# Five tiles of the choice of experts in the first stage instead of six, and five one-hot blocks weighted by VectorE instead of ten

## The reference, cut to what matters

```
x = x + attention(layernorm(x), ctx, ctx)                  # 16 heads, 512 x 512 scores
h = layernorm(x); xn = rmsnorm(h) * norm_w
q = (xn @ wq) as [token, 8 heads, 2, 128]
sim = q . keys                                             # [2, token, head, 64 keys]
s1, i1 = top_k(sim[0], 16);  s2, i2 = top_k(sim[1], 16)
all_scores = s1[:, None] + s2[None, :]                     # 256 per head
final_scores, pk = top_k(all_scores, 16);  final_idx = (i1 * 64 + i2)[pk]
hidden = gelu(xn . expert_down[final_idx]) * relu(final_scores)
x = x + sum over heads and k of hidden * expert_up[final_idx]
```

## Time and profile before

| | |
|---|---|
| median of 3 runs | 1234.25 us (1229.91 to 1236.24) |
| the profiled execution, its span | 1233.31 us, 1231.5 us |
| PE busy | 1062.0 us, 86% |
| PEld busy | 731.2 us, 59% |
| DVE busy | 948.9 us, 77% |
| ACT busy | 393.8 us, 32% |
| POOL busy | 615.3 us, 50% |
| mean granted clock of PE | 0.922 |

### The profile page before, as it was taken

The page is one execution under the profiler, slowest core; times in us unless marked ns, Lnnn a source line. Parts: engine busy times, 40 slices in busy tenths (PEclk is TensorE's granted clock), DMA queues, the critical chain, the costliest instruction groups (busy, mean ns, idle before and its releaser), DMA issues.

```text
span 1231.5 us, 28859 instructions
## 1 busy us (share of the span) xinstructions
PE 1062.0 (86%) x10152; PEld 731.2 (59%) x10152; DVE 948.9 (77%) x4836; ACT 393.8 (32%) x717; POOL 615.3 (50%) x772
## 2 busy tenths in 40 slices
PE   4899987878878777057998999999999999999998
PEld 2444443323212323036787887888878888888887
DVE  4757554968998999669899999998989989953310
ACT  2257544433444353013222222222222222222211
POOL 6320410332210313225777787877877696877511
PEclk9799998888787798556999999999999999999999
DMA  5344313221221110180010000000100010000000
GB/s 166 116 149 143 106 44 121 66 72 49 83 73 47 34 43 6 47 318 3 1 30 16 16 26 17 20 25 11 39 12 25 2 34 16 26 15 24 2 18 9
DMA packets 59924, 63.76 MB, mean 52 GB/s; under 512 B 6882, under 2 KB 56164, under 8 KB 59268
## 3 DMA queue, kind: packets, MB, share of 16 engines
q1 hardware_dynamic: 59780, 61.90, 15.7%
HBM read 42.21 MB, written 19.66 MB: 50 GB/s over the span
## 4 chain that ended last, share of the span: by engine, by line
PE 53%; DVE 27%; POOL 7%; issue 6%; DMA 3%; SPq 2%; ACT 2%; DVEq 0%; POOLq 0%; ACTq 0%
PE bank L1282 50%; DVE mem L1201 4%; PE bank L1285 3%; POOL mem L792 2%; DVE mem L1137 2%; DVE mem L1238 2%; DVE mem L1084 2%; DVE mem L1083 2%; SPq L492 2%; DVE mem L1088 1%; DVE mem L1133 1%; DVE mem L1140 1%; DVE mem L1080 1%; DVE mem L1092 1%; DVE mem L1120 1%
## 5 line engine op out<-in xcount | busy, mean ns | idle before, releaser
L1282 PE MATMUL bank<-mem 128*128 128x32 bf16 (+5 forms) x9672 | 1012.4, 276 | 100.2 <-DVE mem L1201 35.7
L1282 PEld LDWEIGHTS bank<-mem 128*128 128x128 bf16 (+3 forms) x9672 | 679.0, 123 | 382.9 <-issue 175.8
L792 POOL TENSOR_TENSOR mem<-mem 128x1536 bf16<-128x1536 bf16 x118 | 325.7, 2761 | 156.2 <-DVE mem L1235 151.9
L1201 DVE TENSOR_REDUCE mem<-bank 128x1 f32<-128x512 f32 x256 | 167.9, 682 | 87.1 <-PE bank L1282 86.8
L908 ACT ACTIVATE mem<-bank 128x512 f32<-128x512 f32 x256 | 149.0, 601 | 207.9 <-PE bank L1282 207.0
L1238 DVE TENSOR_TENSOR mem<-mem,bank 128x2048 bf16<-128x2048 bf16 x128 | 155.4, 1214 | 0.0
L1285 PE MATMUL bank<-mem 128*128 128x128 f32 (+3 forms) x480 | 75.9, 290 | 66.0 <-POOL mem L704 25.0
L1285 PEld LDWEIGHTS bank<-mem 128*128 128x128 f32 (+3 forms) x480 | 54.9, 142 | 113.8 <-issue 71.0
L799 POOL TENSOR_TENSOR mem<-mem 128x512 f32<-128x512 f32 x64 | 83.5, 1305 | 50.5 <-ACT mem L947 50.5
L958 ACT COPY mem<-bank 128x512 f32<-128x512 f32 x128 | 74.9, 585 | 104.8 <-PE bank L1282 104.8
L673 POOL TENSOR_TENSOR mem<-mem 128x32 f32<-128x32 f32 (+5 forms) x224 | 45.7, 242 | 117.7 <-DVE mem L1092 117.7
(11 more groups left out here) (103 smaller groups left out, 764.1 us busy)
## 6 DMA issues: line engine op xcount, KB each, us to landing
mem<-parts_d SPq DMA_DIRECT2D x192, 64.0 KB, 2.3
parts_d<-mem SPq DMA_DIRECT2D x16, 384.0 KB, 2.6
mem<-in_L_ffn_expert_down SPq DMA_DIRECT2D x16, 256.0 KB, 3.0
downT_d<-mem SPq DMA_DIRECT2D x16, 256.0 KB, 3.2
mem<-downT_d SPq DMA_DIRECT2D x4, 1024.0 KB, 8.5
mem<-in_L_ffn_expert_up SPq DMA_DIRECT2D x4, 1024.0 KB, 16.7
tok_d<-mem SPq DMA_DIRECT2D x16, 160.0 KB, 1.8
mem<-tok_d SPq DMA_DIRECT2D x16, 160.0 KB, 2.4
```

The lines of the kernel that those rows point to most:

```text
L792: nc.gpsimd.tensor_tensor(ow[q % 2], i0, i1, ALU.mult).then_inc(ow_rdy, 1)
L1201: nc.vector.tensor_reduce(nmx[g % 2][:, i % TB, i // TB:i // TB + 1], psum[n % 3][:, :], AX.X, ALU.max, negate=True).then_inc(s_max, 1)
L1282: return nc.tensor.matmul(o, l, r, start=first, stop=last)
```

## The change

NA goes from 6 to 5: tile 5's tasks, similarities, transposition and store leave the first stage, and every wait that counts tiles from NA moves along. The first run of the second stage has five tiles (5 to 9) where it had four (6 to 9); the loop starts at the same tile, 10. OWN keeps the blocks 2, 5, 8, 11 and 14, where it had 1, 2, 4, 5, 7, 8, 10, 11, 13 and 14; POOL weights eleven blocks of the first chunk, where it weighted six.

```diff
         SLOTS = NG + 5
-        NA = 6
+        NA = 5
...
-        OWN = [q for q in range(16) if q % 3 != 0]
+        OWN = [q for q in range(16) if q % 3 == 2]
...
         def runs(eng, run):
-            run(-1, 3, NA, 4, -1)
+            run(-1, 3, NA, 5, -1)
             with eng.Fori(0, 2) as i:
-                run(i * 2 + 2, 2, i * 3 + (NA + 4), 3, None)
+                run(i * 2 + 2, 2, i * 3 + (NA + 5), 3, None)
```

## The result

The changed kernel takes 1254.47 us (median of 4 runs, 1249.45 to 1256.92), the kernel before 1233.89 in the same comparison: 1.0159 times as long, 95% interval 1.0111 to 1.0208. A second comparison, with 6 and 23 runs, gave 1249.1 against 1234.54: 1.0107 (1.0078 to 1.0135). The change makes the kernel slower by 13 to 21 us; forecast were 23 (1257 against 1234), in a range of 1246 to 1267. Both medians lie in the range. The two profiled executions, spans of 1231.5 and 1255.1, are 23.6 us apart.

The account below looks back on a forecast made before the run. DVE was taken to set the time of slots 0 and 1, where it waits only for POOL. -17.4 + 0.9 + 28.6 + 2.4 + 9.6 = +24.1 on 1233.3 gave 1257 us, range 1246 to 1267.

Parts of the forecast that it names:

- Part 1: First stage's tail: without the sixth tile the second stage opens at 504.3 instead of 521.75, -17.4 us.
- Part 3: Slots 0 and 1: a whole tile of choice added, 28.6 work, 2.4 port, 9.6 waits, together +40.6 us.
- Part 2: Slot -1: with five blocks weighted by DVE, POOL's pairs come every 8.0 us instead of 7.81, +0.9 us.
- The bound for a DVE relieved: Slot -1, lower bound: five DVE weightings of 0.87 saved if POOL's pair hid itself, -4.35 us.
- weightings held at the port: Slot -1, upper bound: DVE's five remaining weightings each stand until a POOL weighting ends, +8 us.
- The waits: Slots 0 and 1: DVE's waits for POOL grow from 6.4 to 16.0 us, +9.6 (bounds 0 and 14).
- The port: Slots 0 and 1: the added tile's keys and decoding run slower beside a busy POOL, +2.4 us.
- From slot 2 on: Second stage from slot 2: nothing changes, slots 2 to 7 as before within 1 us each.
- Rival A: Slots 0 and 1: extra waits don't grow because POOL has caught up; sum 1247.8 us; chance 0.16.
- Rival B: Slots 0 and 1: PE, idle a quarter of them, loses clock; +6, 1263 us; chance 0.14.
- Rival C: Slots 0 and 1: PE is the bound and hides DVE's added tile; 1216.8 us; chance 0.04.
- Rival D: Slot -1: DVE's weightings are held by POOL's, +5 to +8 on the sum, 1263 us; chance 0.04.

Follow-up runs that it names:

- the pair with the same clock: Both kernels profiled once more without any edit: 1.0001 (kernel before) and 1.0107 (changed kernel) times the kernel before.
- the edit alone: Kernel before, six tiles kept, with DVE weighting five blocks of the first chunk instead of ten: 1.0010 times the kernel before.
- FEW = 8: Three more searches in slot -1 (FEW was 5): on the changed kernel 1.0101, on the kernel before 1.0031 times the kernel before.
- the exchange: POOL's candidates and expert numbers put ahead of its weighting: on the changed kernel 1.0060, on the kernel before 0.9977 times the kernel before.
- seven tiles: Kernel before with seven tiles of the choice in the first stage and three in the second stage's first run: 1.0104 times the kernel before.

## Why the prediction was right, and where a term was not

The way and the size were right, by its own steps:

- **Part 1, -17.4.** Right: -17.2 by the openings of the pair with the same clock, -17.6 measured from tile 4's decoding. The choice that nothing before the last xn_d store gets earlier held too: it is issued 23.3 us after tile 4's decoding in both kernels. In the first pair of profiles only -10.7 shows, because the changed kernel's execution met half the clock between 150 and 165 us. A forecast made against one profiled execution carries this; it is not part of the change. That the first pair's spans are 23.6 apart, so near the +24.1, is luck: these 6.9 us stand in for the 7.0 that part 3 was too high.
- **Part 2, +0.9.** Right: +0.7 and +0.5, pairs 8.0 us apart as worked out, +0.7 from the edit alone. The bound for a DVE relieved (-4.35) and the one for weightings held at the port (+8) both stayed away: DVE's weighting at 536.41 starts 0.10 before POOL's ends and takes 0.95, as in the kernel before; the longest overlap of the five was 0.32 us, and that one took 1.14.
- **Part 3, +40.6.** Right in kind, too high by 7.0; measured +33.6 (212.5 against 178.9). The work was priced right: DVE is busy for 25.8 us more (196.8 against 171.0), though the keys take 2.6 less beyond their own time, which makes 28.4 of work where 28.6 stood. The waits came where the distances are 1, at choose 2 in four tiles and at the keys in two, 14.1 where 14.6 stood. The three keys at distance 2, put at 1.4, did not wait. Together the waits grew by 7.7 (14.1 less 6.4) where +9.6 stood.

  The port was the step that failed: forecast +2.4 (2.1 of it for the keys), measured -2.6 for the keys (surpluses 5.7 for five tiles, where the four tiles before had 8.3 by rows 9). I had put a surplus on the added tile beside its waits, whatever the distance. But at distance 1 a keys instruction that has waited for the last of POOL's number instructions starts when POOL is idle, since POOL's next weighting needs a one-hot that DVE makes only behind the keys. At 626.94 the wait was 2.38 and the instruction 0.57, and POOL's next weighting came at 629.63. (POOL, then DVE.)

```profile
625.11 1.80 POOL L686 TENSOR_TENSOR mem<-mem 128x128 int32<-128x128 int32 x7
629.63 2.76 POOL L792 TENSOR_TENSOR mem<-mem 128x1536 bf16<-128x1536 bf16 x1 [2.72 <-DVE mem L1235]
```

```profile
626.94 0.57 DVE L1120 SCALAR_TENSOR_TENSOR mem<-mem 128x400 f32<-128x400 f32 x1 [2.38 <-POOL mem L686]
...
629.14 0.41 DVE L1235 TENSOR_TENSOR mem<-mem,bank 128x512 bf16<-128x512 bf16 x1
```

  At distance 2 the next one-hot is already made, and POOL goes from the numbers straight into the weighting: in the kernel before the keys at 639.28 waited 1.01 and then still took 3.12. So the surplus goes with the distance. The two tiles at distance 1 have none in the changed kernel (0.57 to 0.58 us an instruction), the three at distance 2 have 1.9 each, and the four of the kernel before, all at distance 2, had 2.1 each.

  FEW = 8 bears this out: on the changed kernel all five are at distance 1 and none has a surplus, on the kernel before all four are at distance 2 and each has 2.5 or more. With the exchange the trade goes the other way.
- **From slot 2 on**: nothing, within 0.1 us for the four slots together in the first pair and 0.2 in the second.
- **Rival A** (waits don't grow): they grew by 7.7. **Rival B** (the clock): it did fall in slots 0 and 1, to a mean of 0.94 in slot 1, and to 0.50 from 770 to 775. But DVE's own terms make up the whole growth of the two slots, and DVE waits there only for POOL, never for PE, so the clock held nothing up. PE stands idle for 15.2 and 16.6 us, a seventh of the slots and not the quarter that the rival supposed. **Rival C** (PE hides the tile): it needed a growth under 16.5 and there were 33.6. Seen from the other side by seven tiles, C is what happens there. **Rival D** (DVE's weightings held): no, slot -1 grew by 0.7 and 0.5.

The forecast time was 1257, the medians 1254 and 1249. The second pair of spans shows +17.0, so the forecast of +24.1 was 7.1 too high, and part 3 is where nearly all of it lies.

## What to carry to other kernels

Work that moves from a stage's tail to a stage where the same engine is the bound is priced at both ends: by what stood alone in the tail (17.4 of 28.6 us here), and in full where it goes, waits included. The slot without the work shows the other engine's floor, and with it how far a move in the opposite direction pays. Where two engines hand data to and fro in written-out queues, count the steps between producer and consumer before and after: with POOL's candidates and numbers behind its weighting, the waits were 1.3 to 4.2 us at distance 1 (one of 0.04) and 0 to 1.1 at distance 2. And a wait and a port conflict between the same two engines are to be forecast together, from the same count: for the keys distance 1 brought only the wait, distance 2 mostly the conflict, and in part of the tiles both.

## What the runs showed of the hardware that was not expected

The granted clock of PE in the first stage differs between executions of the same instructions. Over the thirteen profiles, whose first stages run the same instructions up to tile 4's decoding, the last instruction of that decoding starts anywhere between 473.8 and 485.3 us, whatever the kernel. A single fall (from 151 to 165 us, 26 matmuls in 10.86 us instead of 5.85) moved everything behind it by 5.9 us. That is half a per cent, as much as the spread of the runs, so a profile's stage should be compared from a common instruction on, not from the span's start. The four latest (483.0 to 485.3) are those whose clock fell to 0.50 between 149 and 165 us or between 270 and 290 us; in the other nine it stood at 1.00 in both stretches. The rows from 270 to 290 us, first of the kernel before in its second profile, then of the kernel before with the exchange:

```profile
270.00:290.00 20.00, 18.90 (x94) 9.58 (x93) 12.62 (x76) 8.83 (x19) 0.65 (x4) 1.00 0.24 76
```

```profile
270.00:290.00 20.00, 19.09 (x57) 9.44 (x58) 5.67 (x29) 4.85 (x12) 0.00 (x0) 0.57 0.14 41
```

What sets off such a fall is open. Before the one at 151 us PE was busy for 4.9 of 5.0 us from 145 to 150 in both executions, at a clock of 1.00, and no experiment was made on it.
